# Second attention: who issues the four transfers that place a half's maxima beside the queries

## The reference, cut to what matters

```python
attn = jnp.einsum('bhqd,bhkd->bhqk', query, key) / scale     # scale = 12
attn = jax.nn.softmax(attn, axis=-1)
out = jnp.einsum('bhqk,bhkd->bhqd', attn, value)
```

## Time and profile before

| | us |
|---|---|
| median of 3 runs | 2129.98 (2129.47 to 2133.92) |
| the profiled execution, its own time | 2124.84 |
| its span in the profile | 2123.1 |
| granted TensorE clock, mean | 0.939 |
| the second attention in it, from the first turn to the end of the last placements | 1237.6 to about 1925 |

### The profile page before, as it was taken

The page is one execution under the profiler, slowest core; times in us unless marked ns, Lnnn a source line. Parts: engine busy times, 40 slices in busy tenths (PEclk is TensorE's granted clock), DMA queues, the critical chain, the costliest instruction groups (busy, mean ns, idle before and its releaser), DMA issues. The chain is left out here.

```text
span 2123.1 us, 32719 instructions
## 1 busy us (share of the span) xinstructions
PE 1816.8 (86%) x12025; PEld 651.2 (31%) x12025; DVE 1473.0 (69%) x3100; ACT 1108.6 (52%) x1385; POOL 633.8 (30%) x771
## 2 busy tenths in 40 slices
PE   6455799999999999999599868888888888887899
PEld 3113333333333333333233312111211211112566
DVE  5874666666666666663344589999999899993543
ACT  4403244454444444445224248778877778885332
POOL 0031445554544454532025003303302400000152
PEclk9776699999999999999799969999999999999699
DMA  4000000000000000000021001111111111103114
GB/s 128 0 1 1 1 12 22 26 27 22 22 22 22 22 22 32 23 27 27 20 107 50 30 8 62 59 42 42 64 55 46 67 47 42 42 27 104 65 32 138
DMA packets 59451, 85.29 MB, mean 40 GB/s; under 512 B 21828, under 2 KB 38468, under 8 KB 59164
## 3 DMA queue, kind: packets, MB, share of 16 engines
q1 hardware_dynamic: 57724, 79.52, 11.1%
q0 software_dynamic: 1280, 2.62, 0.4%
q10 hardware_dynamic: 288, 1.05, 0.2%
HBM read 46.10 MB, written 32.22 MB: 37 GB/s over the span
## 5 line engine op out<-in xcount | busy, mean ns | idle before, releaser
L1575 DVE TENSOR_REDUCE h_m_half<-h_ps_max 128x1 f32<-128x512 f32 x1024 | 637.9, 682 | 53.1 <-PE h_ps_max L1284 49.0
L1460 ACT ACTIVATE h_P<-h_ps_st 128x1024 f32<-128x1024 f32 x512 | 497.7, 1023 | 103.8 <-PE h_ps_st L1300 101.2
L941 ACT ACTIVATE l_P<-l_ps_st 128x1024 f32<-128x1024 f32 (+3 forms) x384 | 306.6, 809 | 293.0 <-PE l_ps_st L821 292.0
L821 PE MATMUL l_ps_st<-l_Q,l_K 64*128 64x512 f32 (+3 forms) x1536 | 330.5, 510 | 1.2 <-DMA l_Q<-l_m_row 1.2
L1019 DVE CUSTOM_DVE_ANT_0 l_masked<-l_ps_t,l_mask 128x384 bf16<-128x384 f32 (+3 forms) x512 | 230.2, 487 | 79.5 <-PE l_ps_t L779 78.0
L1284 PE MATMUL h_ps_max<-h_K,h_Q 48*128 48x512 bf16 x1024 | 205.5, 398 | 78.3 <-DVE h_m_half L1575 75.2
L1310 PE MATMUL h_ps_o<-h_P,h_V 128*9 128x512 f32 x2048 | 271.8, 603 | 0.7 <-ACT h_P L1460 0.5
L1022 DVE TENSOR_REDUCE l_m_half<-l_ps_t 128x1 f32<-128x512 f32 x256 | 164.8, 685 | 97.1 <-PE l_ps_t L779 97.0
L990 POOL TENSOR_SCALAR_AFFINE_SELECT l_P<-l_P 128x256 f32<-128x256 f32 x256 | 102.8, 406 | 381.6 <-ACT l_P L941 381.2
L1300 PE MATMUL h_ps_st<-h_Q,h_K 51*128 51x512 bf16 x1024 | 169.8, 384 | 31.1 <-DMA h_Q<-h_m_row 18.4
L1284 PEld LDWEIGHTS h_ps_max<-h_K,h_Q 48*128 48x128 bf16 x1024 | 49.6, 93 | 404.3 <-DVE h_m_half L1575 385.9
(11 more groups left out here) (387 smaller groups left out, 2207.7 us busy)
## 6 DMA issues: line engine op xcount, KB each, us to landing
sums<-l_o SPq DMA_DIRECT2D x15, 512.0 KB, 2.6
sums<-h_o SPq DMA_DIRECT2D x15, 512.0 KB, 2.6
y_rows<-zero SPq DMA_DIRECT2D x8, 512.0 KB, 4.9
h_b<-h_a SPq DMA_DIRECT2D x32, 128.0 KB, 2.0
c_W<-in_W SPq DMA_DIRECT2D x16, 256.0 KB, 5.6
c_back<-y_rows SPq DMA_DIRECT2D x16, 256.0 KB, 5.4
l_inv<-inverse_sums SPq DMA_DIRECT2D x15, 256.0 KB
l_packed<-sums SPq DMA_DIRECT2D x15, 256.0 KB
```

The lines of the kernel that those rows point to most:

```text
L821: last = pe.matmul(ps_st[x % 2][:, a, 0:w], K[n // NG % 2][rows, kt * 128:(kt + 1) * 128], Q[n % NQ][rows, c, p, q0 - c * CH:q0 - c * CH + ...
L941: act.activation(P[e % PR][:, :, 0:w], ps_st[slot["s", n, i, p] % 2][:, :, 0:w], ACT.Exp, scale=0.125).then_inc(consumed, 1)
L1460: act.activation(P[e % PR][:, :, :], ps_st[x % 2][:, :, :], ACT.Exp, scale=1.0 / 12.0).then_inc(consumed, 1)
L1575: dve.tensor_reduce(m_half[:, half, 2 * p + a, qt:qt + 1], ps_max[:, t % NB, :], AX.X, ALU.max, negate=True)\
```

## The change

The four placing transfers of a turn are issued by ScalarE instead of SP. `turned(h)` calls `place_maxima` itself, directly behind the move of the block out of PSUM; ScalarE waits for its own move to have finished (the same semaphore and the same count that SP waited for), issues the four transfers, and goes on to the exponentials of the step. Sizes, addresses, and the semaphores that the transfers raise are as before. SP's list loses all 32 placements and is otherwise in the same order.

```diff
--- before.py
+++ after.py
@@ -1195,13 +1195,6 @@
                 load_part(sp, S, n, 1)
                 load_part(sp, S, n, 0)
 
-            def place_maxima(n, c):
-                sp.wait_ge(consumed, item["turn", 2 * n + c] + 1)
-                for j in range(HG):
-                    lo, count = 64 * (j % 2) + D6, MP * KT // 2
-                    sp.dma_start(Q[n % NBUF][lo:lo + MP, j // 2, c * CH:(c + 1) * CH].rearrange("x (k c) -> x k c", c=128),
-                                 m_row[c][j * count:(j + 1) * count, :]).then_inc(m_landed[c], 16)
-
             def fetch_sums(n):
                 sp.wait_ge(o_kept, 2 * n + 2)
                 sp.dma_start(sums1[n], o[n % NOB][:, :]).then_inc(sums_stored, 16)
@@ -1223,11 +1216,9 @@
                 sp.dma_start(inv[n // NG % 2][at:at + 32, :], inv1[n].unsqueeze(1).broadcast_to([HG, 8, T])).then_inc(inv_loaded, 16)
                 sp.dma_start(packed[n // NG % 2][at:at + 32, :], sums1[n].rearrange("(j r) t -> j r t", r=32)[:, 0:8, :]).then_inc(o_packed, 16)
 
-            place_maxima(0, 0)
             for n in range(NGR):
                 if n:
                     fetch_sums(n - 1)
-                place_maxima(n, 1)
                 if n % NG < 2 and n // NG + 1 < B:
                     sp.wait_ge(consumed, item[("ka", "x")[n % NG], n // NG + 1, 1] + 1)
                     swap_rows(sp, S, 1 - n % NG)
@@ -1239,8 +1230,6 @@
                     keep_parts(sp, S, n // NG + 1, 0, mixed, n // NG * MIX + MIX)
                 if n + 2 < NGR:
                     load(n + 2)
-                if n + 1 < NGR:
-                    place_maxima(n + 1, 0)
 
         @block.tensor
         def _(pe):
@@ -1412,12 +1401,20 @@
                         act.wait_ge(joined, 2 * b)
                     act.activation(moved[:, cols], ps[:, 0:CH], ACT.Identity, bias=bo[:, b:b + 1], scale=S.mod[:, 1, 2, b:b + 1]).then_inc(consumed, 1)
 
+            def place_maxima(n, c):
+                act.wait_ge(consumed, item["turn", 2 * n + c] + 1)
+                for j in range(HG):
+                    lo, count = 64 * (j % 2) + D6, MP * KT // 2
+                    act.dma_start(Q[n % NBUF][lo:lo + MP, j // 2, c * CH:(c + 1) * CH].rearrange("x (k c) -> x k c", c=128),
+                                  m_row[c][j * count:(j + 1) * count, :]).then_inc(m_landed[c], 16)
+
             def turned(h):
                 act.wait_ge(m_turned, h + 1)
                 if h >= 2:
                     act.wait_ge(m_landed[h % 2], 16 * HG * (h // 2))
                 act.activation(m_row[h % 2][:, :], ps_st[item["turn", h] % 2][0:HG * MP * KT // 2, 0, 0:64].bitcast(BF16), ACT.Identity)\
                    .then_inc(consumed, 1)
+                place_maxima(h // 2, h % 2)
 
             def keep(n, c):
                 act.wait_ge(pv_done, n * NI + (c + 1) * KT)
```

## The result

| | before | after |
|---|---|---|
| median, us | 2130.36 (2129.47 to 2133.92, 4 runs) | 2233.44 (2231.38 to 2236.11, 4 runs) |
| span of the profiled execution, us | 2123.1 | 2229.6 |
| mean granted TensorE clock | 0.939 | 0.921 |

The ratio is 1.048, 95% interval 1.0464 to 1.0497: the changed kernel is slower by 103 us. The prediction had said slower, 2202 us in 2162 to 2236; the sign and the mechanism came out, the size is 31 us short.

What follows compares the result with a forecast made beforehand. VectorE's reductions were taken as the first bound, TensorE second. Turn delays less landing waits 62, long waits 1 and clock 11 make 74 us on 2124.84: 2199, or 2204 on the median; given as 2202, range 2162 to 2236.

Steps and rivals of the forecast that it cites:

- Placement starts no earlier: At the turns, SP's issue already began 0.03 us after ScalarE's move, so moving it to ScalarE gains 0.
- Price of an issue on ScalarE: Behind the move at each turn, four issues hold ScalarE 3.0 us, between 1.8 and 3.1 us, delaying its exponentials.
- 2.6 us for a turn: At steps 6 and 14, late exponentials delay scores and maxima; 16 odd and 15 even turns cost 2.6 us each.
- Turn 0: The first turn costs nothing: ScalarE waits 9.12 us before its first exponential there, and the issues fit in.
- The clock: Behind the new TensorE pauses, 15 of 31 end in the lower clock, less four already there: 11 x 1.0 = 11 us.
- Rival 1: The forecast itself: ScalarE is held as computed at the turns; 2180 to 2215 us on the median, chance 0.72.
- Rival 2: The clock falls after every TensorE pause, each spell costing up to twice 1 us: 2220 to 2247 us, chance 0.12.
- Rival 3: An issue on ScalarE costs 0.445 us or less, 1.8 us for a turn: 2157 to 2164 us, chance 0.07.
- Rival 4: Issues on ScalarE don't hold its exponentials, only the separate queue is left: faster, 2115 us, chance 0.06.
- The gain from the queue: Placements on ScalarE's queue have no load ahead, which can shorten the few long landing waits; the longest was 4.0 us.
- What it would show in the profile: Signs: 0.7 us issues on ACTq, VectorE idle before reductions 115 to 135 us, landing wait under 3 us.

Runs made afterwards that it cites:

- hold: Kernel before, SP still placing, plus ScalarE issuing four same-shaped transfers of a constant into an unused tile at each turn: 2241.28 us, ratio 1.0528.
- fill: Kernel after, plus eight more matmuls of maxima on TensorE at each turn's step, overwritten later: 2207.65 us, ratio 1.0381 to the kernel before.
- odd_spread: Kernel before, but at odd turns ScalarE issues the four placements, one behind each exponential of steps 6 and 7: 2136.75 us, ratio 1.003.
- share_own: Kernel before, but at even turns ScalarE issues two of four placements under exponentials, all four at h = 6, 14, 22 and 30: ratio 1.0019.
- early: Kernel before, with SP's store of parts and load of group n + 2 issued ahead of the inverted sums of group n - 1: 2114.37 us, ratio 0.9923.

## Why the prediction was right, and where its size was off

**Placement starts no earlier: right.** 0.03 us from the move to the issue, as on SP.

**Price of an issue on ScalarE: right.** 0.729 us measured, 3.0 us for four, 3.15 us with the hand-over; taken were 3.0 us from SP's rows. `hold` shows that this time, and nothing in the transfers' new place, is the loss. The Trainium skill ("DMA: Bandwidth & Descriptors", "Issuing engines are not separate DMA queues") calls the issue usually small beside the transfer. Here it is not small, 0.70 or 0.73 us beside a landing 1.2 us behind the last issue, but for one transfer it isn't "the bulk" either, as the prediction put it; for four in a row, 3.0 us, it is.

**2.6 us for a turn: right.** 2.59 and 2.60 us in three of the five intervals without a lower clock at these turns (2.84 and 2.38 in the others), and 2.46 us of idle VectorE in the turn shown. Turn 0 was hidden, as said (interval -0.01 us), and the landing waits went from 18.4 us to none, as the hold swallows them. For the intervals h = 0 to 30 the prediction's terms give 30 x 2.6 - 18.4 = 60 us.

**The clock: the term that was mis-sized.** "I take every second one of 31 to end in the lower clock, 15, less the four that are there: 11 x 1.0 = 11 us." Measured are +99.1 us in these intervals, so 39 us are left for it. Both factors were too small. There were 23 stretches at the lower clock behind the stage's start, not 15, and about half were twice as long, 119 us in all where before had 14. And one cost +0.8 to +1.5 us when short (3.4 to 4.1 less 2.6), +1.9 to +2.8 us when long (4.5 to 5.4 less 2.6). In the 19 intervals with such a stretch and without one of the long landing waits of before, what goes beyond 2.6 us adds up to 32.5 of the 39 us. The 1.0 us came from the pause after one long landing wait, and a single example stood for all. `fill` moves these stretches by nothing but more matmuls, and the price of a turn goes with them, so that the clock has a part in the loss is shown; that it is all of the 39 us is not. A part that is not the clock's alone shows at the turns where the step behind the turn has no first pair of maxima: there the values stand ahead of the maxima. In the kernel after, timeline:

```profile
1495.33 1.89 PE L1299 MATMUL h_ps_o<-h_P,h_V 128*9 128x512 f32 x8
1497.15 0.61 PE L1273 MATMUL h_ps_max<-h_K,h_Q 48*128 48x512 bf16 x2
...
1497.80 2.67 DVE L1572 TENSOR_REDUCE h_m_half<-h_ps_max 128x1 f32<-128x512 f32 x4 [4.79 <-PE h_ps_max L1273]
```

VectorE stands 4.79 us in one piece, 1.89 of it because the values go first and go at 1.2 GHz. I had worked out the two turns of the rows shown, and both have maxima at that place.

The Trainium skill ("TensorE: Matmul & The Clock Gate", "HAM oscillation — how this bites in real kernels") tells of waits of about 3 to 5 us, behind each of which the next group of matmuls begins at the low clock. The pauses here are 2.2 us and less, shorter than those waits, so the page says nothing sure of them; 23 of the 31 turns behind the first had such a stretch all the same, and eight, h = 5, 7 and 24 among them, had none.

**The rivals.** Rival 1 has the mechanism. Rival 2 has its size: it gave 2220 to 2247, from the clock, and the kernel came out at 2233; its condition, the clock falling after every pause, held for 23 of the 31 turns behind the first, and its price, up to twice the 1 us, is about that of the long stretches. The range joined the two. By rival 1 alone, at the most 2215 us, the forecast would have missed by 18 us; that the measured time lies inside, 3 us under the upper bound, is owed to the edge that rival 2 lent, at a chance of 0.12, and so in part to luck. Rival 3 (a cheap issue) falls with 0.729 us. Rival 4 (ScalarE's sequencer only hands the issues over, so that they don't hold it) falls here by the 3.15 us, but `odd_spread` shows half of it true: the sequencer does run beside the engine's work, if work was given to it first. Directly behind the move, which takes 0.27 us and is itself waited for, there is none.

**The gain from the queue: wrong, without weight in the sum.** "The placement's data stood behind the load's on the same queue; on ScalarE's queue nothing stands ahead." Nothing stood ahead in `share_own`, and it landed as late. It is the data under way that counts, and only `early`, which moves the load in time, gets that gain.

**What it would show in the profile.** Idle time before reductions was given as 115 to 135 us and is 149.6; the landing wait as under 3 us and is none.

## What to carry to other kernels

Four small issues are 3 us of their engine: leave them on one that waits anyway, or put each directly behind a long instruction of the engine, where it runs under it. When a pause of TensorE is priced, add what the clock does behind it, counted from several examples at either length. When a small urgent transfer lands late, look for the large one that is under way at the time and move that one; another queue doesn't help.

## What the runs showed of the hardware

- A transfer of 3 KB costs ScalarE's sequencer 0.729 us and SP's 0.699 us; both at once 0.729 and 0.705.
- ScalarE's issue starts with the instruction ahead of it, not behind it, when it doesn't wait for that instruction (1582.07 both), but an instruction behind the issue waits for its end (3.15 us for four).
- A placement landed 1.2 us after its last issue at an odd turn with no load near, and 3.7 to 4.3 us after it (h = 6, 14 and 22) with a load just issued on the other queue. The scores waited about as long for it as on the same queue: 3.66, 3.09 and 3.15 against 3.96, 3.04 and 3.27 us.
- Pauses of TensorE of 2.2 and 0.5 us with two scores in between were followed by the level of 1.2 GHz at 23 of 31 turns; the shorter pauses with two transfers on ScalarE (0.7 and 0.5 us at one turn, 47.2 us of such waits in all) once behind the stage's start; but in `fill`, with 34.2 us of such waits, 21 times.
